# Moving the expansion of the keys to the front of GpSimd's step in an attention and experts kernel

## What is computed

```python
x = x + tanh(g_xattn) * xattn(ctx_1024, layernorm(x), ctx_1024, mask, Wq, Wk, Wv, Wo, bo)
x = x + tanh(g_ffn) * ffn(layernorm(x), shared_w1, shared_w2, expert_w1, expert_w2, router_w, gamma, beta)

# xattn: 16 heads of 8 features; 128 queries and 77 keys per batch
k = einsum('bkhd,ed->bkhe', ctx, Wk); q = einsum('bqhd,ed->bqhe', query, Wq); v = einsum('bvhd,ed->bvhe', ctx, Wv)
product = where(mask == 0, -1e20, einsum('bqhd,bkhd->bhqk', q, k)) / sqrt(8)
out = einsum('bhqv,bvhd->bqhd', softmax(product), v) @ Wo.T + bo

# ffn: one shared expert and the best of 8 experts for every token, with weights quantised to -1, 0, 1 times a scale
```

## Time and profile before

| | before |
|---|---|
| time, median of 3 runs | 556.15 us (555.52 to 556.51) |
| the profiled execution | 558.42 us |
| its span, from the first to the last instruction | 556.6 us |
| TensorE busy | 526.2 us (95%) |
| VectorE busy | 439.7 us (79%) |
| GpSimd busy | 383.7 us (69%) |
| ScalarE busy | 306.7 us (55%) |

### The profile page before, as it was taken

One profiled execution on the slowest core, in us unless ns is written; L12 is line 12 of the kernel. 1 busy time (PEld: TensorE's weight loads), 2 busy tenths in 40 slices (PEclk: granted clock), 3 DMA queues, 4 the chain that ended last, 5 costly groups with the idle time before them and its releaser, 6 DMA issues.

```text
span 556.6 us, 21887 instructions
## 1 busy us (share of the span) xinstructions
PE 526.2 (95%) x8249; PEld 438.7 (79%) x8249; DVE 439.7 (79%) x1270; ACT 306.7 (55%) x683; POOL 383.7 (69%) x864
## 2 busy tenths in 40 slices
PE   6899899999999999999999999999698999999991
PEld 2577687787888888888888888788547999999991
DVE  7687778888888998888777777777776888888871
ACT  3435455555565556657555556445206777777770
POOL 6367867777677786877868777767721777766774
PEclk9799989999999999999999999999688999999996
DMA  6925131021120211202101112000122332222110
GB/s 159 240 71 141 38 108 48 14 63 51 42 63 24 72 44 40 62 24 75 57 29 59 34 42 67 13 17 27 36 79 65 95 91 75 80 84 68 51 40 10
DMA packets 53605, 34.75 MB, mean 62 GB/s; under 512 B 6050, under 2 KB 50926, under 8 KB 53504
## 3 DMA queue, kind: packets, MB, share of 16 engines
q1 hardware_dynamic: 48000, 24.52, 16.5%
q0 software_dynamic: 4352, 8.53, 4.6%
q10 hardware_dynamic: 1152, 0.32, 0.2%
HBM read 24.22 MB, written 9.65 MB: 61 GB/s over the span
## 4 chain that ended last, share of the span: by engine, by line
PE 50%; issue 18%; POOL 16%; DVE 11%; ACT 2%; DMA 1%; POOLq 1%; ACTq 0%; DVEq 0%
PE PS L1155 12%; POOL out L508 9%; PE PS L1123 8%; PE PS L1106 8%; PE PS L1136 7%; PE PS L1093 5%; PE PS L1182 4%; DVE nm L609 3%; DVE rinv L617 2%; POOL rows L463 2%; PE PS L1114 1%; POOL carrier L498 1%; PE PS L1076 1%; ACT shared L942 1%; PE PS L1087 1%
## 5 line engine op out<-in xcount | busy, mean ns | idle before, releaser
L942 ACT ACTIVATE shared<-PS 104x768 f32<-104x768 f32 x128 | 103.7, 810 | 63.6 <-PE PS L1136 63.5
L609 DVE TENSOR_REDUCE nm<-PS 128x8 f32<-128x616 f32 x128 | 101.9, 796 | 27.5 <-PE PS L1106 21.2
L1123 PE MATMUL PS<-xT,kbd 32*104 32x128 f32 x1536 | 117.9, 285 | 0.4 <-ACT shared L942 0.4
L1106 PE MATMUL PS<-kbd,xT 32*128 32x308 f32 x512 | 102.6, 477 | 0.0
L508 POOL DMA_INDIRECT out<-res,tin x72 | 78.0, 1083 | 29.5 <-issue 29.5
L1123 PEld LDWEIGHTS PS<-xT,kbd 32*104 32x104 f32 x1536 | 90.8, 167 | 1.0 <-ACT shared L942 0.9
L617 DVE RECIPROCAL rinv<-PS 128x128 f32<-128x128 f32 x64 | 61.3, 957 | 24.9 <-PE PS L1155 24.0
L463 POOL DMA_INDIRECT rows<-X,pos_i x64 | 66.0, 1031 | 18.7 <-issue 8.4
L1136 PEld LDWEIGHTS PS<-moving,pairsel 128*104 128x104 bf16 x768 | 56.4, 128 | 15.1 <-issue 12.5
L1136 PE MATMUL PS<-moving,pairsel 128*104 128x128 bf16 x768 | 67.0, 224 | 0.0
L1093 PE MATMUL PS<-maskneg,identb 128*128 128x308 bf16 x256 | 55.2, 297 | 3.6 <-DVE nm L609 3.5
(11 more groups left out here) (205 smaller groups left out, 1099.3 us busy)
## 6 DMA issues: line engine op xcount, KB each, us to landing
ctxq<-in_ctx SPq DMA_DIRECT2D x32, 154.0 KB
tin<-rows SPq DMA_DIRECT2D x72, 66.0 KB, 2.0
X<-in_x SPq DMA_DIRECT2D x7, 512.0 KB, 6.7
ctxp<-in_ctx SPq DMA_DIRECT2D x16, 154.0 KB
ctxq<-in_ctx SPq DMA_DIRECT2D x16, 104.0 KB
ctxq<-in_ctx SPq DMA_DIRECT2D x16, 102.0 KB
out<-res,tin POOLq DMA_INDIRECT x72, 2.5
w2n<-in_ew SPq DMA_DIRECT2D x1, 1024.0 KB, 5.9
```

Source lines behind the costliest of these rows:

```text
L609: nc.vector.tensor_reduce(nm[:, b % 2, 2 * u * GH:2 * (u + 1) * GH].rearrange("p (g i) -> p g i", g=2), PS[:, 0:2, 0:GK].rearrange("p g (i ...
L942: nc.scalar.activation(PT[:, b % 2, 2 * u:2 * u + 2, :], PS[0:CR, 2 + 2 * u:4 + 2 * u, 0:CH * P], ACT.Exp, scale=float(1.0 / np.sqrt(HD))) ...
L1106: ins = nc.tensor.matmul(PS[:, v, 0:GK].rearrange("p (i k) -> p i k", k=SK), xT[r, q % 2, j * P:(j + 1) * P], kbd[r, q % 2, j, :, 0:SK], s ...
L1123: nc.tensor.matmul(PS[0:CR, 2 + g, c * P:(c + 1) * P], kbd[r, q % 2, j].rearrange("p i k -> p (i k)")[:, c * CR:(c + 1) * CR], xT[r, q % 2 ...
```

## The change

In GpSimd's program of the attention loop, `expand_keys(b + 3)` becomes the first operation of step b. It stood behind `root(q - 2, 1)` and `make_vm(b - 1)`.

```diff
             for b in range(B + 1):
                 q, j = b // QB, b % QB
+                if b >= 1 and b + QB - 1 < B:
+                    expand_keys(b + QB - 1)
                 if j == 0 and q >= 2:
                     root(q - 2, 1)
                 if 1 <= b < B + 1:
                     make_vm(b - 1)
-                if b >= 1 and b + QB - 1 < B:
-                    expand_keys(b + QB - 1)
                 if j == 3 and q >= 1:
                     root(q - 1, 0)
```

## The result

| | before | after |
|---|---|---|
| time, median of 11 runs each | 556.02 us (553.60 to 558.54) | 552.28 us (550.73 to 555.30) |
| ratio | | 0.9932, 95% interval 0.9909 to 0.9955 |
| the profiled execution, and its span | 558.42 us, 556.6 us | 552.12 us, 550.3 us |
| ScalarE's copy of the keys waits for the expansion | 28.9 us, 14 times | 3.3 us, 2 times |

The change makes the kernel 3.7 us faster; the interval reaches from 2.5 to 5.1 us. No instruction of TensorE, VectorE and ScalarE differs. So the two traces can be laid side by side by one mark that every step has: the start of `transpose_max` (line 1114). In the table a column "3 to 4" is the time from `transpose_max(3)` to `transpose_max(4)`, taken from TensorE's timeline; `transpose_max(t)` runs in step t+1, and "after 63" ends with the span.

What follows compares the result with a forecast made beforehand. TensorE was taken to bound the late attention loop, so only its idle time counted. 0.26 + 1.34 + 1.55 + 0 = 3.15 us off the 556.15 us median gave 553.0 us, range 551.9 to 554.9.

Steps and rivals of the forecast that it cites:

- What bounds: Late attention loop: TensorE busy 60.00 of 60.00 us; ScalarE's 28.9 us of waits count only through TensorE's idle time.
- Step 8: ScalarE's copy of the keys starts 2.23 us earlier, TensorE resumes 1.34 us earlier; with the clock 2.89 us.
- The new bound: In step 9 TensorE waits about half a microsecond for GpSimd's `split_max(8)`.
- the clock's term: Step 9 to 10: the half clock near 70 us goes, 1.55 us gained; the other end is 0.
- Step 4: The expansion gains `make_vm`'s 0.59 us; TensorE's wait of 0.26 us goes, 0.26 us gained.
- Step 12: TensorE's 0.41 us wait goes, but VectorE has no room in step 13: 0 gained, 0.41 us as other end.
- Later quads: All later quads: 0 gained, under TensorE's full occupation or VectorE's lateness.
- The delayed work: `make_vm`, roots and loads come up to 0.70 us later; cost 0, between 0 and a tenth per quad.
- The clock did not fall: Rival: the clock falls all the same near step 9; gain only 1.60 us, 554.55 us; chance 0.20.
- the stall: Rival: timed runs may lack most of the step 8 stall; about 555.6 us; chance 0.10.
- The rival of GpSimd on VectorE: The moved multiplication delays VectorE's operations, up to 0.93 us per quad that VectorE paces; about 557.6 us; chance 0.04.

Runs made afterwards that it cites:

- the idle operations: Changed kernel plus two idle GpSimd memsets ahead of `split_max` in step 8: 552.64 us, ratio 0.9942; with four: 553.25 us, one execution.
- the kernel with first steps only: Against the kernel before, the expansion comes first only where j is 0: 552.16 us, ratio 0.9933.
- the kernel half the way: Against the kernel before, the expansion stands behind the roots and ahead of `make_vm`: 552.33 us, ratio 0.9938.
- the other steps only: Against the kernel before, the expansion comes first only where j is 1, 2 or 3: 554.82 us, ratio 0.9995.
- the two profiles of before: The unchanged kernel before, profiled twice: 558.42 us and 555.49 us.
- the two kernels with the roots behind it: Six root operations of a quad's first step moved behind `split_max`: in the changed kernel 550.94 us (0.9902), in the kernel before 551.85 us (0.9929).

## Why the prediction was right, point by point

**What bounds.** Right as to the place: 28.9 us of ScalarE's waiting were worth 3.4, where TensorE stood idle for it.

**Step 8.** 1.34 us were worked out for the wait and 1.55 for the clock, 2.89 in all; the table shows 14.48 - 11.62 = 2.86, of which 7 to 8 is 7.46 - 6.13 = 1.33 and 8 to 9 is 7.02 - 5.49 = 1.53. The new bound was named (`split_max`, half a microsecond) and is there with 0.48 us. That the clock's term goes was argued from a single wait of 0.64 us; the idle operations show that it was safer than that, up to 1.51 us.

**Step 4.** 0.26 us expected, 0.33 measured: 0.26 was TensorE's idle time, and the other 0.07 us stood in the trace as busy (5.65 of 5.91 us).

**Step 12.** This term was mis-sized: 0 was taken, with 0.41 as the other end, and 0.30 came. The wait goes, and 11 to 12 takes 5.68 us instead of 6.17; VectorE gives part of it back, as forecast, but 12 to 13 takes only 5.66 us instead of 5.47. The prediction held VectorE's chain in step 13 for fixed. It isn't, for the change also turns the order of `make_vm` and the expansion where j is 1, and there line 652 waits on GpSimd. VectorE and GpSimd in step 13 of the changed kernel, against the earlier trace rows:
```profile
89.38 0.62 DVE L652 TENSOR_TENSOR eqb<-eq,best 128x32 bf16<-128x32 f32 x1
```
```profile
89.25 0.70 POOL L367 TENSOR_TENSOR kbd<-kp,rowsel 128x308 f32<-128x308 f32 x1
89.91 0.60 POOL L420 TENSOR_TENSOR vm<-ctxq,own 104x192 f32<-104x192 f32 x1
```
It took 0.62 us, to the end of the expansion, where it had taken 1.12 us, past `make_vm` and to the end of the expansion. In the kernel with first steps only, whose order in step 13 is that of before, it took 1.18 us, and TensorE then waited 0.32 us for VectorE's maxima. So 12 to 13 takes 6.15 us there, and step 13 gets 0.5 us from the part of the change that I had priced at nothing. A loss of the same kind stands in step 12: VectorE's copy of line 713 took 0.21 us before and 0.45 beside the expansion.
```profile
83.28 0.45 DVE L713 COPY free_row<-region 128x8 f32<-128x8 f32 x1
```
In the kernel half the way line 713 takes 0.19 us and line 652 0.56, and it keeps all 0.47 us of 11 to 13; so VectorE had the room that the forecast denied it, and line 713 beside the expansion took part of it up.

**Later quads.** 0 expected; 283.76 and 283.71 us from 13 to 63. The reason given, GpSimd's lighter load behind step 14, was not tested.

**The delayed work.** `make_vm`, the roots and the loads cost nothing that the table shows.

**The rivals.** The clock did not fall. The timed runs had the stall: besides the ratio of 0.9932, their mean granted clock, taken over all of a kernel's runs, is 0.973 to 0.974 before and with the other steps only, and 0.975 to 0.978 in the kernels whose profile has no half clock behind step 9; about half the clock missing over some 3 of 556 us makes 0.0025 (an estimate from the earlier trace rows). The rival of GpSimd on VectorE had its mechanism right and its price wrong: the new order gave 0.5 us at line 652 in step 13 and took 0.24 us at line 713 in step 12. No compare grows to a microsecond; the longest of line 652 is 0.62 us, and the median of line 648 goes from 0.36 to 0.40 us, with 5.78 us from 28 to 29 instead of 5.76. VectorE's busy time in all, 438.9 us, lies between those of the two profiles of before (439.7 and 438.6).

The Trainium skill ("SBUF — State Buffer", Who interferes with whom) says that a VectorE instruction with two inputs in SBUF contends with a GpSimd instruction that reads SBUF. The 0.62 us of line 652 beside the expansion, against 0.19 us in the two kernels where neither the expansion nor `make_vm` falls beside it, agree. Why the 1.12 us of before went on through both instructions it doesn't settle.

**The sum.** 3.15 us expected, 3.44 in the trace, 3.7 in the medians (2.5 to 5.1).

## What to carry to other kernels

A wait of tens of microseconds on an engine that is not the bound is worth only the idle time that it hands on; look for that on the bounding engine, place by place, and price each place with its clock. Where an operation on an in-order engine is moved forward, work out what the same engine then finishes last: here that left half a microsecond, and moving the next operation behind it gave it back. When two operations of GpSimd change places, look at every product of VectorE that falls beside them, in the steps where the move seems to do nothing too.

## What the runs showed that I had not expected

- One wait of up to 1.51 us left TensorE's clock at 1.00; two of 0.39 and 0.65 us with 0.90 us of scores between them brought 1.53 us of loss, in three profiles of three. The same scores with the one wait of 0.65 us behind them cost no clock.
- Line 652 in step 13 got past GpSimd at the end of the expansion where that stood ahead (0.55 to 0.62 us in five profiles), and not at the end of `make_vm` where that stood ahead (1.11 to 1.18 us in five profiles); in the two kernels with the roots behind it met neither (0.19 us). Why it is let in between the two operations in the one order and not in the other is not settled.
- Where TensorE showed 60.00 of 60.00 us, no kernel here is faster: from `transpose_max(44)` to the end of the loop all take 106.05 or 106.06 us. From step 28 to 43 moving the roots still won 0.29 us in the first steps of two quads, where the changed kernel's timeline shows 0.21 and 0.22 us of idle time, and 0.15 us in those of the next two, where it shows none: part of such waiting stands as busy.
